# Moving half of the normalised blocks' transposes, and sharing the last block's normalisation, in an eight-core sandwich layer

## The reference

```
n   = layernorm(x)
qkv = conv1d(n, width 3, 4096 -> 3*1024)
a   = attention in blocks of 128 tokens, 16 heads, causal softmax, with q/k/v/o weights
p   = a @ proj_w + proj_b                  # 1024 -> 4096
x2  = x + layernorm(p)                     # first residual
m   = layernorm(x2)                        # second norm
h   = silu(m gate_w + lora) * (m up_w + lora)     # 4096 -> 11008
y   = h down_w + lora                      # 11008 -> 4096
out = x2 + layernorm(y)
```

## Time and profile before

| what | value |
|---|---|
| time, median of 3 runs | 5141.25 us |
| lowest and highest | 4659.86 and 5208.05 us |
| the profiled execution's own time | 4640.27 us |
| its span on cores 0 to 7 | 4612.2 to 4638.7 us, granted clock 0.976 to 0.979 |
| core 5 (shown below), span | 4638.7 us |
| PE busy (core 0) | 4366.0 us, 94% of the span |
| DVE, ACT busy (core 0) | 1845.5 us (40%), 551.0 us (12%) |

### The profile page before, as it was taken

One profiled execution on the slowest core, in us unless ns is written; L12 is line 12 of the kernel. 1 busy time (PEld: TensorE's weight loads), 2 busy tenths in 40 slices (PEclk: granted clock), 3 DMA queues, 4 the chain that ended last, 5 costly groups with the idle time before them and its releaser, 6 DMA issues.

```text
span 4638.4 us, 57126 instructions; the slowest of 8 cores (4612.2 to 4638.7 us)
## 1 busy us (share of the span) xinstructions
PE 4366.0 (94%) x20743; PEld 1991.2 (43%) x21157; DVE 1845.5 (40%) x3519; ACT 551.0 (12%) x1093; POOL 4.2 (0%) x11
## 2 busy tenths in 40 slices
PE   3899999888999999999999999999899999999994
PEld 2444444433444444444444444444344444344442
DVE  5444444647654555455455555555200000011002
ACT  5200000346100100001001001001000000000001
POOL 0000000000000000000000000000000000000000
PEclk7999999988999999999999999999999999999997
DMA  5244443335344444444444444444655555676655
GB/s 183 82 113 116 114 115 111 128 118 201 123 144 140 138 146 141 135 143 143 137 142 143 140 140 138 143 142 138 199 169 169 166 169 153 186 216 183 184 151 171
DMA packets 255180, 685.81 MB, mean 148 GB/s; under 512 B 25398, under 2 KB 33718, under 8 KB 244022
## 3 DMA queue, kind: packets, MB, share of 16 engines
q1 hardware_dynamic: 241484, 641.29, 46.2%
q10 hardware_dynamic: 13424, 40.85, 2.3%
HBM read 625.94 MB, written 56.10 MB: 147 GB/s over the span
## 4 chain that ended last, share of the span: by engine, by line
PE 90%; DMA 4%; DVE 2%; issue 2%; ACT 1%; SPq 0%; DVEq 0%; POOLq 0%; ACTq 0%
PE bank L512 25%; PE bank L564 24%; PE bank L305 14%; PE bank L486 7%; PE bank L497 6%; PE bank L491 6%; DMA hring<-dn_s 2%; PE bank L455 2%; DVE st L628 1%; PE bank L325 1%; PE bank L389 1%; PE bank L281 1%; PE bank L519 1%; DMA hw<-qk_s 0%; DMA xw<-xs 0%
## 5 line engine op out<-in xcount | busy, mean ns | idle before, releaser
L512 PE MATMUL bank<-xln,usb 128*128 128x512 bf16 x5390 | 1195.8, 379 | 7.7 <-DVE usb L889 1.7
L512 PEld LDWEIGHTS bank<-xln,usb 128*128 128x128 bf16 x5504 | 538.5, 98 | 651.3 <-issue 2.2
L564 PE MATMUL bank<-hid1g,hring 128*128 128x512 bf16 x2692 | 605.6, 380 | 20.4 <-DMA hring<-dn_s 17.2
L564 PE MATMUL bank<-hid0g,hring 128*128 128x512 bf16 x2693 | 604.5, 380 | 14.5 <-DMA hring<-dn_s 11.3
L957 DVE COPY ffn<-bank 128x512 bf16<-128x512 bf16 x64 | 27.1, 424 | 1121.8 <-PE bank L584 1121.8
L564 PEld LDWEIGHTS bank<-hid1g,hring 128*128 128x128 bf16 x2752 | 266.8, 98 | 340.4 <-issue 29.0
L564 PEld LDWEIGHTS bank<-hid0g,hring 128*128 128x128 bf16 x2752 | 267.7, 98 | 333.5 <-issue 20.4
L305 PE MATMUL bank<-vt,raw 128*128 128x512 bf16 x1504 | 359.9, 379 | 4.0 <-DVE gsum L645 2.4
L305 PE MATMUL bank<-vt,gsum 128*128 128x512 bf16 x1506 | 360.0, 379 | 1.6
L887 DVE TENSOR_TENSOR usb<-rawb 128x512 bf16<-128x512 bf16 x344 | 145.4, 423 | 468.3 <-DMA rawb<-gu_s 286.0
L486 PE MATMUL bank<-sx,rawa 128*128 128x512 bf16 x1344 | 322.8, 380 | 2.2 <-issue 0.8
(11 more groups left out here) (131 smaller groups left out, 2702.2 us busy)
## 6 DMA issues: line engine op xcount, KB each, us to landing
hring<-dn_s SPq DMA_DIRECT2D x640, 256.0 KB, 2.8
rawb<-gu_s SPq DMA_DIRECT2D x258, 512.0 KB, 3.7
rawa<-gu_s SPq DMA_DIRECT2D x172, 512.0 KB, 4.4
raw<-conv_s SPq DMA_DIRECT2D x192, 384.0 KB, 3.2
rawb<-gu_s SPq DMA_DIRECT2D x86, 544.0 KB, 3.8
hid_d<-hstage ACTq DMA_DIRECT2D x43, 512.0 KB, 2.7
xw<-xs SPq DMA_DIRECT2D x9, 2048.0 KB, 8.6
xh<-xs SPq DMA_DIRECT2D x16, 1024.0 KB, 6.4
```

The lines of the kernel that those rows point to most:

```text
L512: m = pe.matmul(bank[:, :], u2(n, quad)[:, k * 128:(k + 1) * 128], rhs[:, 4 * i + k, :], start=(i == 0 and k == 0), stop=False)
L564: i = pe.matmul(B[dc % 2][:, :], w[:, ti * 128:(ti + 1) * 128], hch(t, k), start=(k == 0), stop=False)
```

## The change

1. `pe_g_transposes` takes a list of groups. In a block b from 2 on, groups 0 and 1 of block b - 2 stay after piece 1, groups 2 and 3 now come after piece 4.
2. ScalarE's four copies of block b - 2 are split in the same way: two before evacuation 0, two between evacuations 3 and 4.
3. For block 7, ScalarE applies the norm to columns 0 to 2047 only; VectorE writes `tm2` and `tm3` (new semaphore `g_av`). The four copies of block 7 are taken in turn: ScalarE 0 and 2, VectorE 1 and 3. ScalarE changes its table after its half of the apply.
4. The sums `v_sx5` 0 and 1 move from before the residual of block 7 to behind VectorE's half of the apply; the others stand between and behind VectorE's two copies.
5. SyncE's wait before the weight loads of gate/up is for `g_ap` 15 and `g_av` 2 instead of `g_ap` 16.

```diff
--- before.py
+++ after.py
...
@@ -423,10 +423,13 @@
                     pe_av(pe, b - 2, 1)
                 pe_scores(pe, b, 3)
 
-    def pe_g_transposes(pe, b):
-        for grp in range(4):
+    def pe_g_transposes(pe, b, grps):
+        for grp in grps:
             n = b * 4 + grp
-            pe.wait_ge(S["g_ap"], b * 2 + grp // 2 + 1)
+            if b == NB - 1 and grp >= 2:
+                pe.wait_ge(S["g_av"], grp - 1)
+            else:
+                pe.wait_ge(S["g_ap"], b * 2 + grp // 2 + 1)
             if n >= 2:
                 pe.wait_ge(S["gtc"], n - 1)
             for j in range(8):
@@ -456,8 +459,10 @@
                                   start=False, stop=(kc == 7))
                 i.then_inc(S["pjg"], 1)
                 if fb == 1 and b >= 2:
-                    pe_g_transposes(pe, b - 2)
-        pe_g_transposes(pe, NB - 2)
+                    pe_g_transposes(pe, b - 2, (0, 1))
+                if fb == 4 and b >= 2:
+                    pe_g_transposes(pe, b - 2, (2, 3))
+        pe_g_transposes(pe, NB - 2, range(4))
 
 
     def pe_lora_a(pe, t):
@@ -522,7 +527,7 @@
 
     def pe_up(pe):
         pe_lora_a(pe, 0)
-        pe_g_transposes(pe, NB - 1)
+        pe_g_transposes(pe, NB - 1, range(4))
         pe_lora_a(pe, 1)
         for u in range(NU):
             pe_phase1(pe, u, 0)
@@ -797,11 +802,25 @@
                              op=ALU.add).then_inc(S[sem], 1)
 
     def v_act_sums(ve):
+
+        b = NB - 1
+        s, x = st2[b % 2], xh(2 * b + 1)
+        ve.wait_ge(S["g_nm"], b + 1)
+        ve.wait_ge(S["gt"], 4 * b)
+        for q in range(2):
+            ve.tensor_scalar(tm[2 + q][:, :], x[:, q * 1024:(q + 1) * 1024], s[:, 52:53], s[:, 53:54],
+                             op0=ALU.mult, op1=ALU.add).then_inc(S["g_av"], 1)
+        ve.wait_ge(S["gtc"], 16)
+        ve.wait_ge(S["pjg"], NB * 8)
+        v_sx5(ve, 0)
+        v_sx5(ve, 1)
+        ve.wait_ge(S["gtc"], 4 * NB - 3)
+        g_copy(ve, ve.tensor_copy, NB - 1, 1)
         v_sx5(ve, 2)
+        ve.wait_ge(S["gtc"], 4 * NB - 1)
+        g_copy(ve, ve.tensor_copy, NB - 1, 3)
         v_sx5(ve, 3)
-        ve.wait_ge(S["gtc"], 24)
         v_sx12(ve, 0, 256, "sx")
-        ve.wait_ge(S["gtc"], 28)
         v_sx12(ve, 256, 384, "sx")
         ve.wait_ge(S["gtc"], 32)
         v_sx12(ve, 384, 512, "sy")
@@ -820,11 +839,6 @@
 
     def v_proj(ve):
         for b in range(NB + 1):
-            if b == NB:
-                ve.wait_ge(S["gtc"], 16)
-                ve.wait_ge(S["pjg"], NB * 8)
-                v_sx5(ve, 0)
-                v_sx5(ve, 1)
             if b > 0:
                 v_residual(ve, b - 1)
             if b < NB:
@@ -1039,12 +1053,15 @@
             sc.wait_ge(S["f_add"], 2 * (b - 1) + fb // 4 + 1)
         sc.copy(attn[:, fb * 512:(fb + 1) * 512], B[e % 6][:, :]).then_inc(S["ev"], 1)
 
-    def s_g_copies(sc, b):
+    def g_copy(eng, copy, b, grp):
         t, off = b // 4, (b % 4) * 128
-        for grp in range(4):
-            sc.wait_ge(S["gt"], b * 4 + grp + 1)
-            sc.copy(xln2[t][:, grp * 8:(grp + 1) * 8, off:off + 128],
-                    BT[6 + grp % 2].rearrange("p (c t) -> p c t", t=128)).then_inc(S["gtc"], 1)
+        eng.wait_ge(S["gt"], b * 4 + grp + 1)
+        copy(xln2[t][:, grp * 8:(grp + 1) * 8, off:off + 128],
+             BT[6 + grp % 2].rearrange("p (c t) -> p c t", t=128)).then_inc(S["gtc"], 1)
+
+    def s_g_copies(sc, b, grps):
+        for grp in grps:
+            g_copy(sc, sc.copy, b, grp)
 
     def s_g_apply(sc, b, h):
         i = b * 2 + h
@@ -1060,26 +1077,30 @@
         k.then_inc(S["g_ap"], 1)
 
     def s_proj(sc):
-        for b in range(NB + 1):
+        for b in range(NB):
             if b >= 2:
                 if b == 6:
 
                     sc.wait_ge(X2[3], 32)
-                s_g_copies(sc, b - 2)
-            if b < NB:
-                for fb in range(6):
-                    s_evac(sc, b, fb)
+                s_g_copies(sc, b - 2, (0, 1))
+            for fb in range(4):
+                s_evac(sc, b, fb)
+            if b >= 2:
+                s_g_copies(sc, b - 2, (2, 3))
+            for fb in range(4, 6):
+                s_evac(sc, b, fb)
             if b > 0:
                 s_sqrt(sc, "g", b - 1, st2[(b - 1) % 2])
-            if b < NB:
-                s_evac(sc, b, 6)
+            s_evac(sc, b, 6)
             if b > 0:
                 s_g_apply(sc, b - 1, 0)
-            if b < NB:
-                s_evac(sc, b, 7)
-                s_sqrt(sc, "f", b, st[b % 2])
+            s_evac(sc, b, 7)
+            s_sqrt(sc, "f", b, st[b % 2])
             if b > 0:
                 s_g_apply(sc, b - 1, 1)
+        s_g_copies(sc, NB - 2, range(4))
+        s_sqrt(sc, "g", NB - 1, st2[(NB - 1) % 2])
+        s_g_apply(sc, NB - 1, 0)
 
     def s_last_shift(sc, t, g, h):
         n = t * 4 + g
@@ -1108,7 +1129,10 @@
                      hs[p % 2].rearrange("p (t f) e -> p t (f e)", t=2)).then_inc(HD[p % 2], 16)
 
     def s_up(sc):
-        s_g_copies(sc, NB - 1)
+
+        g_copy(sc, sc.copy, NB - 1, 0)
+        sc.wait_ge(S["gtc"], 4 * NB - 2)
+        g_copy(sc, sc.copy, NB - 1, 2)
         sc.wait_ge(S["f_add"], 16)
         for u in range(NU):
             if u % 2 == 1:
@@ -1268,7 +1292,8 @@
                         sy.wait_ge(S["pjg"], 32)
                     y_x_load(sy, i + 4)
 
-        sy.wait_ge(S["g_ap"], 16)
+        sy.wait_ge(S["g_ap"], 15)
+        sy.wait_ge(S["g_av"], 2)
         sy.wait_ge(X2[3], 64)
         for u in range(NU):
             for i in range(2):
```

More of the change, by code:

```diff
@@ L225, in build_nc @@
              "cg cge vg vge pbu pbc sc mx ex rc pn pt ptc av avc wog woe "
-             "pjg ev f_bn f_ag f_va f_sd f_ri f_nm f_add g_bn g_ag g_va g_sd g_ri g_nm g_ap gt gtc "
+             "pjg ev f_bn f_ag f_va f_sd f_ri f_nm f_add g_bn g_ag g_va g_sd g_ri g_nm g_ap g_av gt gtc "
              "sx sy xa xc xs xac m5 m2 c1 c2 s1 s2 r5 r2 ma mb k1 k2 fa fb f1 f2 si hid hring xd xdc dns dnt dntc j_bn j_ag j_va j_sd j_ri j_nm j_sh j_x j_res").split()
```

## The result

| | before | change |
|---|---|---|
| median of 9 runs each, us | 4989.11 | 4619.82 |
| lowest, us | 4639.27 | 4615.88 |
| profiled execution, us | 4640.27 | 4617.84 |
| ratio, with 95% interval | | 0.9931 (0.9914 to 0.9947) |
| down stage starts, mean of 8 cores, us | 3301.2 | 3275.3 |

The ratio says 0.7% faster: under the 2% that counts as a difference, but clear of 1. A second comparison of the same two kernels gave 0.9961 (0.9938 to 0.9983). Some executions of either kernel run with one die at a lower clock, and the ratio leaves them out; the medians don't, so only the ratio compares the kernels.

What follows compares the result with a forecast made beforehand. The prediction took TensorE to bound the kernel nearly everywhere. Gains of 20.3 us in blocks 2 to 7 and 3.4 at the stage's end, 23.7 off 4640.3, gave 4617 us, range 4598 to 4666.

Steps and rivals of the forecast that it cites:

- TensorE's wait for ScalarE goes, and nothing takes its place: Blocks 2 to 7: the waits at transposes vanish, ScalarE keeps about 1 us of slack, a block takes 17.7 us.
- rival 1: Blocks 2 to 7: ScalarE or VectorE sets the pace, 19.0 us a block, 6.5 us lost, 4623 us; 12%.
- rival 4: Blocks 2 to 7: freed time becomes a new wait at piece 5 or 6, only the stage's end gains, 4637 us; 4%.
- The reference point: Whole kernel: 23.7 us taken off the profiled execution's 4640.3 us, giving 4617 us, 0.5% less.
- the blocks' term: Blocks 2 to 7 of the projection: stalls and slow matmuls go, gaining 20.3 us, 13 at the bottom.
- Rival 2: Blocks 2 to 7: the clock falls at each of twelve transpose visits, 2.9 us each, 11 us slower, 4651; 6%.
- The end: Block 7 to phase 2: shared norm and copies and moved sums gain 3.4 us, bounds 1.7 to 4.3.
- R: End of the stage: the moment when residual 7 can begin, 0.34 us after the reciprocal, 1151.43 us before.
- VectorE as the last to arrive: End of phase 1: VectorE's sums end at R + 29.2, 1.6 us after the LoRA product at R + 27.6.
- A term put at nothing: Down stage: no term in the sum; only the blocks and the stage's end counted, 23.7 us.
- rival 3: Gate/up: it starts earlier only to wait for weights from shared memory, the gain is hidden, 4640 us; 8%.

Runs made afterwards that it cites:

- Experiment 3: As experiment 1, but ScalarE makes all four copies of a block ahead of evacuation 0: first transposes to phase 2 155.3 to 156.4 us, blocks 106.3.
- experiment 2: The change with transposes of blocks 2 to 7 back in one place after piece 1, copies ahead of evacuations: first transposes to phase 2 mean 169.2 us, profiled 4640.77.
- experiment 6: The change with a block's four transpose groups after pieces 1, 2, 4 and 5: first transposes to phase 2 145.75 to 146.0 us.
- experiment 4: As experiment 1, all transposes after piece 4, four copies between evacuations 3 and 4: first transposes to phase 2 151.7 to 153.1 us (157.5 to 158.9 to compare).
- experiment 1: The kernel before with only parts 1 and 2, the split transposes and copies: first transposes to phase 2 149.7 to 150.5 us, profiled 4619.25.
- experiments 7 and 8: 7: the change, block 7's copies on ScalarE, sums early: first transposes to phase 2 mean 144.8 us. 8: 7 with phase 2 waiting by quarters: 142.7.

## Why the prediction was right, and where not

The forecast was 4617 us, and the median came out at 4619.8, in the range. The mechanism was right and the difference too; what failed is the time from which the difference was taken, and two terms have another size. By its steps:

- **TensorE's wait for ScalarE goes, and nothing takes its place**: right. No wait is left in the blocks. A block takes 17.3 us, and VectorE's residuals are 17.0 to 17.7 us apart, so VectorE lies just under it, and ScalarE's slack sufficed (rival 1 is false, and so is rival 4). Experiment 3 shows what it would have cost if not.
- **The reference point: the step that failed.** The prediction took 23.7 us off one profiled execution of 4640.3 and gave an absolute time, 4617 us. It saw that the median on record was 5141.25, and it named its 0.5% only against the one execution; read against that median, 4617 says 10% faster. The runs showed 0.7% and 0.4% (0.9931 and 0.9961), against executions of the kernel before of 4639 to 4660 us. Nothing in the kernel could have brought the other 501 us. The forecast to state was a ratio of 0.995.
- **Size of the blocks' term**: forecast 20.3, measured 22.4 on core 5, and 19.1 to 27.0 on the eight, mean 22.9. Two errors. Eight transposes at full pace were taken as 0.54 us from a row behind a wait; 16 take 0.89 between matmuls, which is 2.3 us over six blocks. And the slow pairs were read on one core, where they cost 3.6 us over their full pace; across the cores they cost 1.0 to 7.4, and with slower transposes they make the blocks 119 to 127 us long. Which cores and blocks they hit differs between the kernel before and experiment 2, the two kernels that keep the wait.
- **Rival 2, the clock at each visit**: false. Pairs behind all 12 visits (the change) and all 24 (experiment 6) ran at the full level on every core, and so did the transposes: 16 put the next instruction back by 0.89 us. The Trainium skill (TensorE: Matmul & The Clock Gate, Part 4: PE-mode transpose) says that a transpose doesn't run at the full clock level and doesn't count as busy in the same way. The first half of this doesn't agree with the 0.89 us. The second half stays open, since no run parts it: slow pairs stood only behind visits that took 4.5 to 5.5 us from the first transposes to the next matmuls (transposes and waits together), and not each time; none stood behind visits of 3.2 us (experiment 4) or of 1.0 us and less.
- **The end**: phase 2 at R + 41.75 for R + 41.7. The new TENSOR_SCALAR take 0.73 us each by their starts, near the lower bound, and were hidden as said. Forecast 3.4, measured 3.3 on core 5, and 3.9 to 4.8 against experiment 1. VectorE as the last to arrive: right on all eight cores, by 0.27 us instead of 1.6 on core 5, since the LoRA product ran 9.8 us there and not 8.6. The parts agree too: VectorE's second copy ends at R + 19.2 for 18.9, and its cast starts at R + 29.25 for 29.2.
- **A term put at nothing: the down stage.** The stretch is 26.5 us shorter in the mean and the down stage starts 25.9 us earlier, but takes 5.5 us longer. The slowest core before (5) started it at 3302.8 and the slowest of the change (0) at 3276.9; it took 1335.9 and 1339.4, and this leaves the 22.4 us that the profiled execution lost. So 22.4 lies near the forecast of 23.7 by luck in part: 2 to 3 us more were gained in the stage and as much given back behind it.

The down stage's extra time is waiting for its weights. The pages of core 0, before and then the change, show it:

```profile
L564 PE MATMUL bank<-hid1g,hring 128*128 128x512 bf16 x2692 | 605.6, 380 | 20.4 <-DMA hring<-dn_s 17.2
L564 PE MATMUL bank<-hid0g,hring 128*128 128x512 bf16 x2693 | 604.5, 380 | 14.5 <-DMA hring<-dn_s 11.3
...
L569 PE MATMUL bank<-hid1g,hring 128*128 128x512 bf16 x2692 | 606.5, 380 | 24.0 <-DMA hring<-dn_s 20.9
L569 PE MATMUL bank<-hid0g,hring 128*128 128x512 bf16 x2693 | 603.1, 380 | 15.0 <-DMA hring<-dn_s 12.0
```

In the mean of eight cores these waits are 25.1 us before and 30.4 in the change. Most of the difference is two cores of the kernel before: cores 6 and 7 waited 16 us and their down stages took 1314 and 1320, while those of the other six took 1332 to 1340, and the change's eight took 1333 to 1341. Over all twelve profiles the means are 1331 to 1341, lowest in the two kernels whose down stage starts last (the kernel before and experiment 2). Whether cores that arrive earlier and closer together wait longer, or this is scatter, stays open: no run parts the two. Up to the down stage rival 3 is false: the first L517 waits for VectorE, and not for weights.

## What to carry to other kernels

If TensorE's side work (transposes into two banks) waits for an engine that is in order, ask what stands ahead of that engine's answer: moving the work to a place where the answer is ready gave 14.5 us, and splitting it so that the copies lie under matmuls 8.4. Without the same split on the answering engine 6.2 us of them are lost. A wait of TensorE among transposes can cost more than its own length, through a lower clock in the matmuls behind it, and differently on each core; read all cores before sizing it. State a forecast for a small change as a ratio to the executions that it was worked out from, not as a time. At the end of a stage, put work on the last-arriving engine in the order in which its inputs are ready (experiments 7 and 8 found 3 us more).

## What the runs showed of the hardware

- Visits to transposes with 2.05 to 2.57 us of idle time in them were followed by 16 matmuls in 3.6 to 6.1 us, slow ones in 27 and 29 of 48 cases (the kernel before, experiment 2). Visits with waits of 0.8 and 0.3 us, or a wait of 0.97 us ahead of a piece, were followed by none above 3.63 us for 16, on all eight cores (experiments 4, 3).
- VectorE's TENSOR_SCALAR of 1024 columns, f32 to bf16, started its successor after 0.73 us. A SCALAR_TENSOR_TENSOR of 2048 columns with two f32 inputs and f32 output took 2.3: 1.6 times as long per column.
- Without waits the six blocks took the same time on eight cores within 0.01 us.
- TensorE's waits for the down stage's weights were 16 to 33 us per core in the kernel before and the change, and the stage's length follows them: over the 96 cores of the twelve profiles the correlation of the two is 0.87.
